# Attention and FFN on one core: the token phase by single tiles in 21 steps, and the transform as whole 512x512 products

## The reference

```python
# x: 4 batches x 2048 tokens x 512, float32; 16 heads of 32
q, k, v = x @ Wq.T + bq, x @ Wk.T + bk, x @ Wv.T + bv            # by heads
scores = q @ k.T / sqrt(32) + bias     # bias: -inf on 3 columns chosen from band_importance
y = x + softmax(scores) @ v @ Wo.T + bo
attn = layernorm(y) * gamma + beta
x1 = layernorm(x + attn)
xh = x1 @ H                            # H: Hadamard 512x512, divided by sqrt(512)
s = clip(max(abs(xh)), 1e-5) / 7       # per token
xq = clip(round(xh / s), -8, 7) * s    # 4 bits
out = layernorm(x1 + xq @ wq.T)        # wq: weight made ternary, one scale per row
```

## Time and profile before

| | us |
|---|---|
| median of 3 runs | 5915.57 (5913.42 to 5923.06) |
| profiled execution, its own time | 5918.79 |
| its span, first to last instruction | 5916.7 |

### The profile page before, as it was taken

How to read it: one execution, slowest core, us unless ns; L and a number is a source line. 1 busy time by engine, 2 the same in 40 slices (tenths; PEclk the granted TensorE clock), 3 DMA queues, 4 the chain that set the end, 5 groups by cost and what they waited for, 6 DMA issues and landing times.

```text
span 5916.7 us, 89211 instructions
## 1 busy us (share of the span) xinstructions
PE 5113.6 (86%) x25133; PEld 2540.5 (43%) x25161; DVE 3822.4 (65%) x6400; ACT 2444.1 (41%) x4698; POOL 3058.0 (52%) x909
## 2 busy tenths in 40 slices
PE   6999999985599999997569999999657999999954
PEld 3444444433344444443334544444334444444422
DVE  4666565658575757575856665657684757575768
ACT  0445454531154545453125454545213545454511
POOL 1555565652165656564226565656323756565622
PEclk8999999987799999998789999999778999999976
DMA  5323223221313141412121323232213141413121
GB/s 120 71 59 72 59 61 67 52 60 50 73 36 86 33 86 33 86 33 67 54 65 36 84 47 72 49 74 46 61 46 78 33 86 33 86 33 86 33 72 43
DMA packets 255591, 358.52 MB, mean 61 GB/s; under 512 B 17009, under 2 KB 104849, under 8 KB 255122
## 3 DMA queue, kind: packets, MB, share of 16 engines
q1 hardware_dynamic: 255122, 352.81, 26.3%
HBM read 212.67 MB, written 33.55 MB: 42 GB/s over the span
## 4 chain that ended last, share of the span: by engine, by line
PE 72%; DVE 11%; DMA 10%; issue 3%; ACT 3%; SPq 1%; POOL 0%; ACTq 0%; DVEq 0%; POOLq 0%
PE ps_m L436 20%; PE ps_s L451 17%; PE ps_o L476 15%; DMA qst<-lo 6%; PE ps_z L456 4%; PE ps_m L422 4%; PE ps_m L403 3%; PE ps_m L411 3%; DMA xk<-in_xT_dram 3%; PE ps_s L501 2%; DVE stats L742 2%; PE ps_m L515 1%; SPq L257 1%; PE ps_s L515 1%; ACT prob L604 1%
## 5 line engine op out<-in xcount | busy, mean ns | idle before, releaser
L706 DVE TENSOR_REDUCE umax<-ps_m 128x1 f32<-128x512 f32 x4160 | 2565.3, 683 | 715.5 <-PE ps_m L436 715.5
L604 ACT ACTIVATE prob<-ps_s 128x512 f32<-128x512 f32 x4096 | 2125.0, 601 | 1650.1 <-PE ps_s L451 1429.2
L900 POOL TENSOR_TENSOR acc<-acc,prob 128x2048 f32<-128x2048 f32 x512 | 2345.9, 4582 | 454.3 <-ACT prob L604 430.5
L451 PE MATMUL ps_s<-qst,kst 99*128 99x512 f32 x4096 | 1694.4, 429 | 129.0 <-ACT prob L604 76.4
L436 PE MATMUL ps_m<-kst,qst 97*128 97x512 f32 x4160 | 1726.4, 423 | 30.6 <-DMA qst<-lo 30.6
L451 PEld LDWEIGHTS ps_s<-qst,kst 99*128 99x128 f32 x4096 | 759.3, 189 | 1206.6 <-ACT prob L604 660.4
L476 PE MATMUL ps_o<-prob,vst 128*32 128x512 f32 x8192 | 1092.0, 605 | 0.0
L436 PEld LDWEIGHTS ps_m<-kst,qst 97*128 97x128 f32 x4160 | 793.3, 191 | 471.5 <-DVE umax L706 331.7
L900 POOL TENSOR_TENSOR acc<-prob 128x2048 f32<-128x2048 f32 x64 | 293.0, 4578 | 741.0 <-ACT prob L604 741.0
L686 DVE SCALAR_TENSOR_TENSOR lo<-ps_m,bias,hi 128x512 fp32r<-128x512 f32 x134 | 100.6, 751 | 777.6 <-ACT hi L583 456.0
L884 POOL TENSOR_TENSOR obuf<-obuf,zinv 128x512 f32<-128x512 f32 x64 | 82.1, 1283 | 911.7 <-DVE zinv L719 911.7
(11 more groups left out here) (106 smaller groups left out, 2534.9 us busy)
## 6 DMA issues: line engine op xcount, KB each, us to landing
xk<-in_xT_dram SPq DMA_DIRECT2D x70, 1024.0 KB, 8.8
xq<-in_xT_dram SPq DMA_DIRECT2D x67, 1024.0 KB, 8.8
kst<-hi SPq DMA_DIRECT2D x136, 256.0 KB, 10.3
qst<-hi SPq DMA_DIRECT2D x132, 256.0 KB, 5.6
kst<-lo SPq DMA_DIRECT2D x68, 256.0 KB, 10.0
wq<-in_wT_dram SPq DMA_DIRECT2D x67, 256.0 KB, 9.4
qst<-lo SPq DMA_DIRECT2D x66, 256.0 KB, 6.8
ctxT_dram<-obuf SPq DMA_DIRECT2D x64, 256.0 KB, 2.6
```

The lines of the kernel that those rows point to most:

```text
L451: nc.tensor.matmul(ps_s[:, (i * HG * NKC + HG * c + h) % NSB, :], kst[i // NQB % 2][0:RALL, h, c * P:(c + 1) * P], qst[i % 2][0:RALL, h, : ...
L604: nc.scalar.activation(prob[:, c % NPB, h, :], ps_s[:, (i * HG * NKC + HG * c + h) % NSB, :], ACT.Exp, scale=SCALE).then_inc(ex, 1)
L706: nc.vector.tensor_reduce(umax[:, m, kb:kb + 1], ps_m[:, u % NMB, :], AX.X, ALU.max).then_inc(mred, 1)
L900: nc.gpsimd.tensor_tensor(acc[:], a, prob[:, c % NPB], ALU.add).then_inc(padd, 1)
```

## The change

The token phase becomes a pipeline of single tiles in 21 steps (22 on those engines that begin with step -1). Each step is a loop of one turn, written out for each s. In step s VectorE handles the sum of tile s, layernorm 1 and 2's parts of tile s-1, the maximum of tile s-3, and the last add of tile s-4; the reciprocal roots of the three layernorms (of tiles s-1, s-2 and s-5) are worked out together, on three columns. ScalarE applies layernorms 2 and 3 (Identity with scale and bias columns) and quantises: it scales and adds the rounding constant, then takes it off again. No clipping is left, since |xh / s| is at most 7. VectorE writes three of its results back into PSUM in place (`ps_wo`, `ps_f`). The multiplication by gamma goes from GpSimd to VectorE, joined with the subtraction of the mean; scaling and adding x + beta are one operation. The transform is one product with the whole 512x512 matrix, four float32 products of 512 columns, with the transposed tile as the stationary side; its four blocks (1 MB) are loaded at the start of each token phase. VectorE's sums and differences of halves (L806 to L811) go.

```diff
+NT = L // P
+LN1, LN2, LN3 = range(3)
+AGE = {LN1: 1, LN2: 2, LN3: 5}
+STEPS = NT + AGE[LN3]
+NST = 3
+def step_of(eng, b):
+    return eng.Fori(b, b + 1)
...
# SP
+                for c in range(IC):
+                    sp.dma_start(had_sb[c], had[c * P:(c + 1) * P, :]).then_inc(had_ld, 16)
...
+                for t in range(2):
+                    with step_of(sp, b) as bb:
+                        load_rows(bb, t)
+                        load_context(bb, t)
+                for s in range(-1, STEPS):
+                    with step_of(sp, b) as bb:
+                        if 0 <= s + 1 < NT - 2:
+                            wait_alone(sp, c_xg, bb * NT + (s + 2), passed)
+                            load_rows(bb, s + 3)
+                            wait_alone(sp, c_wo, bb * NT + (s + 2), passed)
+                            load_context(bb, s + 3)
+                        if 0 <= s - AGE[LN3] < NT:
+                            store(bb, s - AGE[LN3])
...
# TensorE
+                for s in range(-1, STEPS):
+                    with step_of(pe, b) as bb:
+                        t = s + 1
+                        if t < NT:
+                            pe.wait_ge(c_ldc[t % 2], bb * (NT // 2 * 16) + (t // 2 + 1) * 16)
+                            if t >= 3:
+                                pe.wait_ge(c_y, bb * NT + (t - 2))
+                            for h in range(NG):
+                                mm = nc.tensor.matmul(ps_wo[t % 3], tC[t % 2][:, h * P:(h + 1) * P], wo_sb[:, h, :],
+                                                      start=h == 0, stop=h == NG - 1)
+                            mm.then_inc(c_wo, 1)
+                        t = s - 3
+                        if 0 <= t < NT:
+                            pe.wait_ge(c_q, bb * NT + (t + 1))
...
+                                mm = nc.tensor.transpose(ps_qt.bitcast(BF16)[:, c * P:(c + 1) * P],
+                                                         tQB[t % 2][:, c * P:(c + 1) * P], identb[:])
+                            mm.then_inc(c_qt, 1)
+                            pe.wait_ge(c_qtc, bb * NT + (t + 1))
...
+                                mm = nc.tensor.matmul(ps_f[t % 2], tQT[t % 2][:, c * P:(c + 1) * P], ternT[:, c, :],
                                                       start=c == 0, stop=c == IC - 1)
                             mm.then_inc(c_ffn, 1)
+                        t = s - 2
+                        if 0 <= t < NT:
+                            pe.wait_ge(c_x1, bb * NT + (t + 1))
...
+                                mm = nc.tensor.transpose(ps_ht[:, c * P:(c + 1) * P], tY[t % 4][:, c * P:(c + 1) * P], ident[:])
+                            mm.then_inc(c_wt, 1)
+                            pe.wait_ge(c_wtc, bb * NT + (t + 1))
+                            if t >= 1:
+                                pe.wait_ge(c_q1, bb * NT + t)
+                            for c in range(IC):
+                                mm = nc.tensor.matmul(ps_h, tHT[t % 2][:, c * P:(c + 1) * P], had_sb[c],
+                                                      start=c == 0, stop=c == IC - 1)
+                            mm.then_inc(c_h, 1)
...
# ScalarE, step s
+                            nc.scalar.activation(lnv[:, s % 2, cols, 0], mv[:, cols, 1], ACT.Sqrt, bias=eps[:]).then_inc(c_sd, 1)
...
+                            nc.scalar.activation(tY[t % 4], tY[t % 4], ACT.Identity, scale=lnv[:, s % 2, LN2, 1:2],
+                                                 bias=lnv[:, s % 2, LN2, 4:5]).then_inc(c_x1, 1)
...
+                            act.wait_ge(c_sc, bb * NT + (t + 1))
+                            nc.scalar.activation(tQ, ps_h, ACT.Identity, scale=qsc[:, t % 2, 2:3], bias=magic[:]).then_inc(c_q1, 1)
...
+                            nc.scalar.activation(tQB[t % 2], tQ, ACT.Copy, bias=-MAGIC).then_inc(c_q, 1)
...
+                            nc.scalar.activation(tQT[t % 2], ps_qt.bitcast(BF16)[:, 0:D], ACT.Copy).then_inc(c_qtc, 1)
...
+                            nc.scalar.activation(tO[t % NST], tO[t % NST], ACT.Identity, scale=lnv[:, s % 2, LN3, 1:2],
+                                                 bias=lnv[:, s % 2, LN3, 4:5]).then_inc(c_o, 1)
...
+                            nc.scalar.activation(tHT[t % 2], ps_ht, ACT.Copy).then_inc(c_wtc, 1)
...
# VectorE, step s; q, f, y = s - 3, s - 4, s - 1
+                            nc.vector.tensor_tensor(ps_wo[s % 3], ps_wo[s % 3], tXB[s % 2], ALU.add).then_inc(c_sum, 1)
...
+                            dve.wait_ge(c_sd, bb * (STEPS - 1) + s)
+                            mark(nc.vector.reciprocal(r, sd))
+                            own()
+                            mark(nc.vector.tensor_tensor(a, r, r, ALU.mult))
+                            own()
+                            mark(nc.vector.scalar_tensor_tensor(out=w, in0=var, scalar=LN_EPS, in1=a, op0=ALU.add, op1=ALU.mult))
+                            own()
+                            mark(nc.vector.tensor_scalar(w, w, -0.5, 1.5, ALU.mult, ALU.add))
+                            own()
+                            mark(nc.vector.tensor_tensor(r, r, w, ALU.mult))
+                            own()
+                            nc.vector.scalar_tensor_tensor(out=nb, in0=mean, scalar=-1.0, in1=r, op0=ALU.mult, op1=ALU.mult)\
+                                .then_inc(c_rs, 1)
...
+                            dve.wait_ge(c_h, bb * NT + (q + 1))
+                            nc.vector.tensor_reduce(qsc[:, q % 2, 0:1], ps_h, AX.X, ALU.max, apply_absolute_value=True)\
+                                .then_inc(c_mx, 1)
...
+                            nc.vector.scalar_tensor_tensor(out=ps_f[f % 2], in0=ps_f[f % 2], scalar=qsc[:, f % 2, 1:2],
+                                                           in1=wscale[:], op0=ALU.mult, op1=ALU.mult).then_inc(c_fs, 1)
...
+                            mark(nc.vector.tensor_scalar(qsc[:, q % 2, 1:2], qsc[:, q % 2, 0:1], 1e-5, 1.0 / 7.0, ALU.max, ALU.mult))
...
+                            nc.vector.scalar_tensor_tensor(out=ps_wo[y % 3], in0=ps_wo[y % 3], scalar=mv[:, LN1, 0:1], in1=gam,
+                                                           op0=ALU.subtract, op1=ALU.mult).then_inc(c_ng, 1)
...
+                            nc.vector.reciprocal(qsc[:, q % 2, 2:3], qsc[:, q % 2, 1:2]).then_inc(c_sc, 1)
...
+                            nc.vector.tensor_tensor(tO[f % NST], ps_f[f % 2], tY[f % 4], ALU.add).then_inc(c_fo, 1)
...
+                            nc.vector.scalar_tensor_tensor(out=tY[y % 4], in0=ps_wo[y % 3], scalar=lnv[:, s % 2, LN1, 1:2],
+                                                           in1=tXG[y % 3], op0=ALU.mult, op1=ALU.add).then_inc(c_y, 1)
...
+                            mark(nc.vector.bn_stats(stats[:, LN1, :], ps_wo[s % 3]))
...
+                            mark(nc.vector.bn_stats(stats[:, LN3, :], tO[f % NST]))
...
+                            mark(nc.vector.bn_stats(stats[:, LN2, :], tY[y % 4]))
+                        for k in norms_of(s + 1):
+                            if k == norms_of(s + 1)[0]:
+                                wait_alone(dve, c_dve, bb * total + marks[0], passed)
+                            nc.vector.bn_aggr(mv[:, k, :], stats[:, k, :]).then_inc(c_mv, 1)
...
# GpSimd, step s; t = s + 1
+                            pool.wait_ge(c_ldx[t % 2], bb * (NT // 2 * 16) + (t // 2 + 1) * 16)
+                            if t >= 2:
+                                pool.wait_ge(c_sum, bb * NT + (t - 1))
+                            nc.gpsimd.tensor_tensor(tXB[t % 2], tX[t % 2], bob, ALU.add).then_inc(c_xb, 1)
+                            if t >= 3:
+                                pool.wait_ge(c_y, bb * NT + (t - 2))
+                            pool.wait_ge(c_xb, bb * NT + (t + 1))
+                            nc.gpsimd.tensor_tensor(tXG[t % 3], tX[t % 2], bet, ALU.add).then_inc(c_xg, 1)
```

More of the change, by code:

```diff
@@ L75, in wait_alone, with norms_of, moments_by, stored_by @@
     eng.sem_inc(passed, 1)
[L78 to L86 removed]
+def step_of(eng, b):
+    return eng.Fori(b, b + 1)
+def norms_of(s):
+    return [k for k in (LN1, LN2, LN3) if 0 <= s - AGE[k] < NT]
+def moments_by(s):
+    return sum(len(norms_of(r)) for r in range(s + 1))
+def stored_by(k, t):
+    return len([i for i in range(t) if i % NST == k])
+def batch_done(eng, c_st, b, passed):
+    for k in range(NST):
+        wait_alone(eng, c_st[k], b * (16 * stored_by(k, NT)) + 16 * stored_by(k, NT), passed)
 def build(nc, x, xT, wT, bqkv, woT, w_ffn, band, gamma, beta, bo, had, out):
@@ L336, in tokens @@
[L336 to L347 removed]
+                wait_alone(sp, q_stk, (b * NBLK + NBLK + 2) * NSTK, passed)
@@ L380, in _ @@
                 tokens(b)
-            sp.wait_ge(c_st, NS * NQB * 16)
+            for k in range(NST):
+                sp.wait_ge(c_st[k], NB * 16 * stored_by(k, NT))
             sp.wait_ge(wkv_ld, (NS + 2) * 32)
```

379 lines of the change are left out of this document (130 added, 249 removed).

## The result

The changed kernel takes 5725.89 us (median of 4 runs, 5723.98 to 5734.83), the kernel before 5917.08 us in the same comparison (4 runs). The ratio is 0.968, with a 95% interval of 0.966 to 0.970: 3.2% faster, 191 us. The prediction said 5715, between 5683 and 5800. The profiled execution of after took 5726.64 us, its span 5724.8 us, its mean granted clock was 0.968 (before: 0.932).

The account below looks back on a forecast made before the run. The prediction took VectorE to bound the token phases. Start, filling, 15 periods of 11.4 us and draining gave 50.5 us gained a phase, 202 in four: 5717 profiled, 5715 us median, range 5683 to 5800.

Parts of the forecast that it names:

- The ring's members: Token-phase step: maximum, scale, ScalarE's scaling and rounding, transposes, copies, last product and transform follow in a loop setting the period.
- The period, 11.4: Token phase: one tile every 11.4 us in the pipeline, against 15.4 in the kernel before.
- 4.19: Steady step: time from the transform's end through VectorE's maximum and scale and ScalarE's rounding to the bfloat16 transposes, 4.19 us.
- 7.03: Steady step: time from the bfloat16 transposes through copies and last product to the transform's end, 7.03 us.
- The 0.2 us for waits: Steady step: allowance for waits on two semaphores, between 0 and 0.9 us, taken as 0.2.
- the cheap end: VectorE's three results written to PSUM: priced like operations that read PSUM and write SBUF, 0.75 us.
- The rival at +0.7: VectorE's three PSUM writes cost 0.7 us more each: period 12.8, total 5806 us; chance 0.10.
- the 9.9: VectorE's work for each tile in the token phase, port stall included: 9.9 us, against 13.4 before.
- the port stall: VectorE's tiny operations wait for GpSimd's addition on the shared SBUF port: 1.1 us a tile.
- The low clock: Rival for the token phase: TensorE stays at 1.2 GHz, period 18.5 us, total 6185 us; chance 0.05.
- 0.95 or more but for its first 7 us: Sign to look for: TensorE's granted clock over the token phase, apart from its start.
- the forecast end of 1521.3: First token phase: VectorE ends at 1521.3, where it ended at 1571.8 before; gain 50.5 us a phase.

Follow-up runs that it names:

- 4: Changed kernel with two of the four products of each output projection left out; 5812.6 us (one run).
- 8: Changed kernel with the last operation of layernorms 2 and 3 moved back from ScalarE to VectorE; 5728.84 us (one run).
- 6: Kernel before, still in pairs, with the whole 512x512 matrix in place of VectorE's sums and differences of halves; 5930.87 us, ratio 1.0021.
- 5: Changed kernel with sums and differences of halves back on VectorE and the 128x128 block in place of the 512x512 matrix; 5676.91 us (one run).
- 1: Changed kernel with three unused projections added in steps 15 to 17 to keep TensorE busy; 5688.73 us, ratio to before 0.9605.
- 9: Changed kernel with both the halves and the last operation of layernorms 2 and 3 back on VectorE; 5735.07 us (one run).
- 10: Changed kernel with halves back on VectorE, quantising scale worked out first, both GpSimd additions held until VectorE's two-operand work is done; 5579.67 us, ratio 0.9428.

## Why the prediction was right, and where its terms were off

**The bound and the mechanism: right for after, half right for before.** A ring through all three engines sets the step after. The ring's members were those forecast, and 4 (TensorE's work cut, same step) and 8 (VectorE's work grown, same step) show that it is the ring and no engine's load. Of before the prediction said that VectorE is the bound. VectorE's part of the pair's chain goes from the projection's end to L511, 1441.30 to 1460.15, 18.9 of the 30.8 us; the rest is TensorE's and ScalarE's. The pair was a ring too, and VectorE only the larger part of it: in 6, which takes 5.3 us off VectorE and gives TensorE a longer transform, the pair stays as long.

**The period, 11.4 against 10.91.** From the transform's end to the bfloat16 transposes the prediction had 4.19, the chain has 3.82 (1403.42 to 1407.24): neighbours on VectorE overlap, so L788 and L794 advance the queue by 0.66 and 0.65 (their starts to those of what follows them), not 0.77. From the transposes to the transform's end it had 7.03, the chain has 7.09. The 0.2 us for waits were not there. Twelve steps from 1338.93 to 1468.92 took 130.0, not 136.8: 6.8 us better than forecast.

**PSUM writes: the cheap end was right.** Timeline of VectorE in the steady step:

```profile
1404.05 0.75 DVE L788 SCALAR_TENSOR_TENSOR ps_m<-ps_m,qsc,wscale 128x512 f32<-128x512 f32 x1
...
1404.77 0.75 DVE L794 SCALAR_TENSOR_TENSOR ps_s<-ps_s,mv,acc 128x512 f32<-128x512 f32 x1
```

0.75, as L790 took when it wrote SBUF. The rival at +0.7 falls.

**ScalarE: right.** With two column operands 0.78 was estimated; L653 took 0.777, and L648 and L665, which read SBUF, 0.81 and 0.80. Groups of after by form:

```profile
L653 ACT ACTIVATE prob<-ps_m,magic,qsc 128x512 f32<-128x512 f32 x64 | 49.7, 777 | 248.1 <-DVE qsc L798 248.1
...
L644 ACT ACT_TABLE_LOAD x4 | 5.1, 1283 | 0.1
```

Four table loads at L644 in four phases, so none between Identity and Sqrt within a phase; the Trainium skill (ScalarE: Activation LUTs, "Table sets: the hidden batching unit") says that identity is in every set, and the trace agrees.

**VectorE's load: the 9.9 was too high.** 72.79 us in 108 is 7.4 us for each step of 10.91. The overlap of neighbours is one part. The other is the port stall, charged at 1.1 in every step. It is there while the pipeline fills and all but gone in the steady steps:

```profile
1324.29 1.27 DVE L773 SCALAR_TENSOR_TENSOR lnv<-mv,lnv 128x1 f32<-128x1 f32 x1
...
1330.29 1.29 DVE L771 TENSOR_TENSOR lnv<-lnv 128x2 f32<-128x2 f32 x1
...
1410.05 1.28 POOL L916 TENSOR_TENSOR prob<-lo,acc 128x512 f32<-128x512 f32 x1 [1.79 <-DVE ps_s L758]
...
1410.78 0.18 DVE L769 RECIPROCAL lnv<-lnv 128x3 f32<-128x3 f32 x1 [0.81 <-ACT lnv L644]
1410.99 0.36 DVE L771 TENSOR_TENSOR lnv<-lnv 128x3 f32<-128x3 f32 x1
```

In the steady step VectorE must first wait 0.81 us for ScalarE's root, which is queued behind the copy L672; the addition (1410.05 to 1411.33) passes during that wait, and L771 is stretched by 0.19. What the prediction missed is that the stall and the wait lie over each other. The term was wrong by 0.9 us and cost nothing, since VectorE had slack. Where it had none, in 5, the stall was full. The Trainium skill (SBUF — State Buffer, "SBUF: two separate sides") has the pair of SBUF ports that VectorE and GpSimd share locked for a whole instruction; the trace agrees for three columns as for 256, and 5 shows that two stalls in one step do occur.

The prediction named this stall for the new kernel alone. The kernel before paid it as well, inside the busy time of VectorE. Its chain in order of time:

```profile
1456.40 1.48 DVE prob L806
1457.89 1.42 DVE prob L807
...
1459.67 0.43 DVE prob L811
```

L806 and L807 are of the same size as L811 and stand beside GpSimd's additions of bo (L907, 1456.26 to 1459.01). So some of the 26.8 us of a pair were waits for GpSimd, 2.1 us in these two operations. No run holds GpSimd back in the order of before.

**The low clock: the step of the argument that failed.** It was weighed as a ring that stays at 1.2 GHz or does not. What came was a ring at 2.4 GHz whose last three steps lose it. The forecast "0.95 or more but for its first 7 us" is wrong: from 1320.5 to 1523.1, without the first 7 us, it is 0.92 (1.00 up to 1471, 0.68 behind it), and 0.87 over the phase with its loads. Two readings led there: the longest gap of 0.7 us was that of the steady step, with the projection in it, and the drain was counted at the same period; and the earlier trace rows were one gap in an otherwise busy stretch, which 4 shows to be no measure. Term: 9.9, 10.1, 7.4 and 7.7 us in the four phases, shown by 1 (10.91 in these steps and 10.39 in the last when the projections go on).

**Filling, draining, restarting.** The first projection starts at 1313.46 (forecast 1313.9). From there to the first maximum, at 1338.93, it is 25.5 us (forecast 26). The way from the last transform to ScalarE's last output is 11.6 us (1511.46 to 1523.07; forecast 10.4). The last product ends 5.6 us after the transform, as forecast (1517.09), but VectorE's L788 starts only at 1517.83, behind the six tiny operations of its step, and from there to the end it is 5.2 us and not 4.8. The end of the phase, in the chain:

```profile
1523.30 2.02 DMA out_dram<-prob
1525.32 5.16 issue
```

The step back to attention takes 5.16 us instead of the 4.11 that were to stay. Over the first three phases it was 4.11, 4.83 and 4.25 before, 5.16, 5.09 and 5.18 after: some 0.75 us a phase more, and 4.8 to 5.5 behind the first phase in the experiments with the pipeline (4.15 in 6, which has pairs). Its cause stays open; no run changed the loops alone.

**The sum.** Against the forecast end of 1521.3: -0.4 start, -0.5 filling, -6.8 twelve steps, +8.4 the last three (42.6 against 34.2), +1.2 draining, which gives 1523.2 (measured 1523.07). The first phase with its restart ends 1578.20 - 1530.48 = 47.7 us earlier than before; the second and third bring 45.0 and 47.3 us, the last, which has no restart, 51.9. Together that is the difference of the spans, 5916.7 - 5724.8 = 191.9. So 5715 was 11 us too low for the last steps and the restart. That it came so near is luck in part: the ring forecast too long (6.8 us a phase) and the clock forecast too good (8.4 in the first phase) nearly cancelled.

**What the gain is made of.** The change was weighed as work taken from VectorE. The runs say otherwise: 183 us come with the pipeline even when the halves and the two normalisations stay on VectorE (9), ScalarE's normalising adds 58 on top (9 to 5), and the whole matrix takes 49 of that back (5 to after). In the order of before the matrix gave nothing either (6). How the 183 us divide between the order and the work that 9 still saves VectorE is not shown. The prediction never priced the parts alone and could not see this.

## What to carry to other kernels

When the work of a tile goes round several engines, write down the ring with each engine's order, and shorten that; work moved between engines pays only where the mover's engine is the ring's or the step's bound, and the next bound may lie half a microsecond below. Count the last steps of a pipeline separately: the filler that keeps TensorE's clock up ends there first, and a product counted at 2.4 GHz then takes longer (here 5.6 to 6.2 us for 3.7). An engine's stall by GpSimd is a matter of timing, and a wait that moves GpSimd's work can remove it (10).

## What the runs showed of the hardware that was not expected

- A hole of 2.1 us in every step of 11 to 14 us took TensorE's granted clock to 0.81 over 108 us (4), and holes of 3.8 us in the last steps to 0.61 and 0.66; one gap of 2.5 us in a busy stretch had left it at 1.00. Filling the holes of the last steps with unused products brought 0.66 over 40 us back to 0.94 (1).
- VectorE writing PSUM in place over 512 columns costs what writing SBUF does: 0.75 us.
- One addition of GpSimd stretches a VectorE operation of three columns from 0.17 to 1.29 us (5); beside the same additions the statistics (L814 and L817: 0.68) and a reciprocal (L769: 0.18) kept their times in after.
- Loops of one turn at each step cost nothing that the chain shows: the steady ring has no piece for them.
